# A transformer block on one core: the split for the fourth projected tile of a slot goes behind one more addition, and its cast waits for that addition

## The reference

```python
h = _ln(x, g1, be1)
x = _attn(h, h, Wq1, Wk1, Wv1, Wo1, bo1) + x     # self-attention
h = _ln(x, g2, be2)
x = _attn(h, context, Wq2, Wk2, Wv2, Wo2, bo2) + x
h = _ln(x, g3, be3)
y = h @ Wp + bp
a, gate = (y[..., :FF_HID], y[..., FF_HID:])
x = a * jax.nn.gelu(gate, approximate=False) @ W2 + b2 + x
```

## Time and profile before

| | |
|---|---|
| median of three runs | 2030.56 us (2029.66 to 2030.76) |
| the profiled execution | 2030.76 us, of which 2029.0 us are the span from first to last instruction |
| busy shares of the span | TensorE 99%, VectorE 69%, ScalarE 58%, GpSimd 73% |
| the six slots with projections | from 441 us to 1235 us |

### The profile page before, as it was taken

How to read it: one execution, slowest core, us unless ns; L and a number is a source line. 1 busy time by engine, 2 the same in 40 slices (tenths; PEclk the granted TensorE clock), 3 DMA queues, 4 the chain that set the end, 5 groups by cost and what they waited for, 6 DMA issues and landing times.

```text
span 2029.0 us, 32337 instructions
## 1 busy us (share of the span) xinstructions
PE 2015.9 (99%) x12692; PEld 1387.4 (68%) x12692; DVE 1392.1 (69%) x2128; ACT 1186.6 (58%) x1895; POOL 1476.3 (73%) x785
## 2 busy tenths in 40 slices
PE   8999999999999999999999999999999999999999
PEld 7665665667565566765665666565558999888888
DVE  5588677666767785577678566758777888744443
ACT  5566566665557675465667555557665666533332
POOL 2599899989979998999799889979894576300000
PEclk9999999999999999999999999999999999999999
DMA  7300000001000000010000001000020520000100
GB/s 230 125 27 22 6 6 16 6 27 48 16 12 6 17 7 27 1 63 6 6 6 22 26 1 52 6 27 1 22 60 5 146 84 1 1 22 22 42 11 32
DMA packets 48183, 64.01 MB, mean 32 GB/s; under 512 B 6048, under 2 KB 41504, under 8 KB 46368
## 3 DMA queue, kind: packets, MB, share of 16 engines
q1 hardware_dynamic: 48032, 61.96, 9.6%
HBM read 43.07 MB, written 18.87 MB: 31 GB/s over the span
## 4 chain that ended last, share of the span: by engine, by line
PE 96%; POOL 2%; issue 1%; ACT 1%; DMA 1%; DVE 0%; SPq 0%; POOLq 0%; ACTq 0%
PE score L516 21%; PE score L499 18%; PE score L641 9%; PE score L503 6%; PE attn_project L655 5%; PE score L447 4%; PE attn_project L627 4%; PE score L597 4%; PE attn_project L447 4%; PE first_score L473 3%; PE score L459 3%; PE attn_project L473 2%; PE score L565 1%; PE attn_project L459 1%; PE first_score L540 1%; PE attn_project L565 1%
## 5 line engine op out<-in xcount | busy, mean ns | idle before, releaser
L1392 POOL TENSOR_TENSOR acc<-acc,pT 128x1024 f32<-128x1024 f32 x384 | 916.2, 2386 | 53.6 <-POOL acc L1389 0.4
L1146 ACT ACTIVATE pT<-score 128x1024 f32<-128x1024 f32 x512 | 525.3, 1027 | 153.4 <-PE score L503 112.2
L499 PE MATMUL score<-qk 64*128 64x512 f32 x3072 | 457.2, 399 | 1.5 <-ACT oT L1159 0.9
L516 PE MATMUL score<-pT,vT 128*64 128x512 f32 x2016 | 446.5, 595 | 0.0
L818 DVE TENSOR_REDUCE nmax<-first_score 128x1 f32<-128x512 f32 x512 | 349.4, 682 | 4.8 <-PE first_score L473 2.9
L818 DVE TENSOR_REDUCE nmax<-attn_project 128x1 f32<-128x512 f32 x512 | 348.7, 681 | 0.0
L499 PEld LDWEIGHTS score<-qk 64*128 64x128 f32 x3072 | 257.8, 184 | 118.2 <-ACT pT L1146 65.9
L516 PEld LDWEIGHTS score<-pT,vT 128*64 128x64 f32 x2016 | 139.2, 137 | 289.3 <-issue 251.8
L840 DVE RECIPROCAL sums<-sums 128x512 f32<-128x512 f32 (+1 forms) x65 | 214.4, 3299 | 53.8 <-ACT sums L1193 53.2
L503 PE MATMUL score<-shift,pick 64*128 64x512 f32 x1024 | 206.2, 391 | 0.0
L1389 POOL TENSOR_TENSOR acc<-pT 128x1024 f32<-128x1024 f32 x64 | 154.0, 2406 | 68.9 <-ACT pT L1146 68.9
(11 more groups left out here) (170 smaller groups left out, 3086.9 us busy)
## 6 DMA issues: line engine op xcount, KB each, us to landing
xres<-x_middle SPq DMA_DIRECT2D x10, 512.0 KB, 3.8
xres<-in_x SPq DMA_DIRECT2D x4, 1024.0 KB, 8.7
raw_qk<-in_L_xattn_Wq SPq DMA_DIRECT2D x32, 128.0 KB, 2.3
raw_qk<-in_L_xattn_Wk SPq DMA_DIRECT2D x32, 128.0 KB, 2.4
raw_v<-in_L_xattn_Wv SPq DMA_DIRECT2D x8, 512.0 KB, 4.1
keys_all<-keys SPq DMA_DIRECT2D x1, 4096.0 KB, 12.1
values_all<-values SPq DMA_DIRECT2D x1, 4096.0 KB, 12.4
out_x<-xres SPq DMA_DIRECT2D x7, 512.0 KB, 2.9
```

The costliest lines, as they stand in the source:

```text
L499: e.matmul(bank, qk[P % 2][r, 2 + h, keys], qk[P % 2][r, w, queries], start=(part == 0), stop=False)
L516: last = e.matmul(banks[bank][head * DH:(head + 1) * DH, :], vT[:, v_slot(D, jt), c0:c0 + DH], pT[:, jt, head, :], start=(jt == 0), stop=( ...
L1146: e.activation(pT[:, jt].rearrange("p h n -> p (h n)"), SC[R % 2][:, :], ACT.Exp).then_inc(s.exponential, 1)
L1392: e.tensor_tensor(total, total, pT[:, jt], ALU.add).then_inc(s.probs_added, 1)
```

## The change

It has three parts, all for tile 3 of a slot. On ScalarE its cast, which waited for tile 0's projection alone, now also waits for `attended` at 8C + 7 and `probs_added` at 7C + 6. On GpSimd its subtraction waits for `attended` at 8C + 8 and no longer for tile 0's projection. And GpSimd does that subtraction after add 6 instead of after tile 2's.

```diff
@@ split_oT of ScalarE
-                if j < 3:
-                    need.wait_ge(s.attended, TILES * C + 2 * j + 1)
-                    need.wait_ge(s.probs_added, (TILES - 1) * C + max(2 * j, 1))
-                else:
-
+                need.wait_ge(s.attended, TILES * C + 2 * j + 1)
+                need.wait_ge(s.probs_added, (TILES - 1) * C + max(2 * j, 1))
+                if j == 3:
                     need.wait_ge(s.out1_product, TILES * b + t - j + 1)
@@ split_oT of GpSimd
                 need.wait_ge(s.oT_hi, TILES * b + t + 1)
-                if j < 3:
-                    need.wait_ge(s.attended, TILES * C + 2 * j + 2)
-                    need.wait_ge(s.probs_added, (TILES - 1) * C + 2 * j + 1)
-                else:
-                    need.wait_ge(s.out1_product, TILES * b + t - j + 1)
+                need.wait_ge(s.attended, TILES * C + 2 * j + 2)
+                need.wait_ge(s.probs_added, (TILES - 1) * C + 2 * j + 1 if j < 3 else 0)
@@ the loop of GpSimd over the chunks
-                    for tile in out1_tiles(C)[{4: slice(0, 2), 5: slice(2, 4)}.get(jt, slice(0, 0))]:
+                    for tile in out1_tiles(C)[{4: slice(0, 2), 5: slice(2, 3), 6: slice(3, 4)}.get(jt, slice(0, 0))]:
                         split_oT(C, *tile)
```

## The result

| | before | after |
|---|---|---|
| median of the runs | 2030.62 us (2029.66 to 2030.76, 4 runs) | 2047.11 us (2046.39 to 2049.41, 4 runs) |
| ratio, 95% interval | | 1.0084 [1.0066, 1.0102] |
| the profiled execution, its span | 2030.76 us, 2029.0 us | 2048.4 us, 2046.6 us |
| mean granted clock of TensorE | 1.000 | 0.997 |

The change costs 16.5 us, 0.8%. The forecast was 2045.2 in a range of 2041 to 2048.5. The median lies in the range, but the clock is not at 1.000 as forecast.

What follows compares the result with a forecast made beforehand. TensorE was taken as the bound; its new waits for tile 3's low part in six slots sum to 14.41 us, so 2030.76 + 14.41 = 2045.2 us, 0.7% slower, in a range of 2041 to 2048.5.

Steps and rivals of the forecast that it cites:

- TensorE bounds the stage and gives nothing back: Self-attention stage: TensorE waits only 2.5 us in all; at most 1.6 us could be regained, none taken.
- The rival of stalls given back: Score phase: ScalarE runs ahead after stalls, each chunk returning up to 1.3 us; not slower, 2030.8; chance 4%.
- The redundant conditions cost nothing: Tile 3's split: added waits for attend 7 or 8 cost nothing; dropping GpSimd's wait for tile 0's product gains nothing.
- The wait makes cast and subtraction serial behind add 6: Tile 3, six slots: cast and subtraction follow add 6 in turn, making TensorE 1.12 to 3.31 us late.
- The sum of 14.41: Lateness of tile 3's projection on TensorE in C = 17, 18, 33, 34, 49 and 50, 14.41 us together.
- What is late next: GpSimd after tile 3's subtraction: it falls less behind than TensorE, its V weights split does not wait; no second stall.
- The clock: Rival: TensorE's clock halves after gaps of about 3 us in C = 18, 34, 50; 8.6 more, 2053.8; chance 5%.

Runs made afterwards that it cites:

- the move alone: Changed kernel, but ScalarE's cast for tile 3 waits only for add 4 and tile 0's projection; 2036.60 us, ratio 1.0032.
- the run with the gap filled: Changed kernel plus 24 extra TensorE matmuls ahead of its wait for tile 3 in C = 18, 34 and 50; 2043.61 us, ratio 1.0066.
- the second slots: Kernel before, with the whole change only in C = 18, 34 and 50; 2042.41 us, ratio 1.0060.
- the redundant conditions undone: Changed kernel, but tile 3 waits for no `attended` and GpSimd's subtraction again for tile 0's projection; 2047.10 us, ratio 1.0084.
- first slots alone: Kernel before, with the whole change only in C = 17, 33 and 49; 2034.60 us, ratio 1.0021.
- a third filled: Changed kernel plus 8 extra TensorE matmuls ahead of its wait for tile 3 in C = 18, 34 and 50; 2045.83 us, ratio 1.0078.

## Why the prediction was right, and where it was not

*TensorE bounds the stage and gives nothing back.* Right. Lateness and slow matmuls, counted from the starts, account for the growth of the span to 0.1 us. The rival of stalls given back is refuted: the weight loads waited 64.8 us in 362 waits for exponentials in the changed kernel, against 65.9.

*The redundant conditions cost nothing.* Right, by the run that undoes them (2047.10 against 2047.11).

*The wait makes cast and subtraction serial behind add 6.* Right in mechanism: the cast's releaser is the add. With the move alone 6.3 us remain.

*The sum of 14.41.* It measured 13.2. From the start of tile 2's subtraction to tile 3's projection in C = 17 I had 8.58 us; it took 458.89 - 450.48 = 8.41. The hand-over from the add to the cast was 0.03 and not 0.08, the one to TensorE 0.10 and not 0.14, and an operation of GpSimd follows the one before it 0.03 before that one's recorded end. Six times 0.2 is the difference.

*What is late next.* Wrong in a detail that costs nothing. GpSimd's split of V weights does wait for the projection after C = 18 (1.32 us in the changed kernel), since the projection was slower than the 2.87 that I took. In the run with the gap filled, where it was not slow, GpSimd goes from the scaling to that split without a pause. GpSimd is behind nobody there.

*The clock.* This step failed. I gave the fall 5% and took none; it happened, in three of three long stalls of the profiled execution, at 5.7 us in all. My price of 8.6 was near it in kind, a projection at half speed, but only in C = 34 was nearly all of the projection slow. The argument against it was the 3.27 us of idle time before the first matmul, with the clock at 1.00 in the window around it. I misread that. The timeline of before goes on like this:

```profile
5.19 6.11 PE L391 MATMUL score<-ctxT,wkv 128*128 128x256 f32 x16 [0.38 <-DVE ctxT L790]
11.14 1.89 PE L391 MATMUL attn_project<-ctxT,wkv 128*128 128x256 f32 x8
12.87 1.89 PE L391 MATMUL score<-ctxT,wkv 128*128 128x256 f32 x8
```

The first 16 matmuls take 11.14 - 5.19 = 5.95 us, 0.37 each. The next ones, of the same line and shape, take (12.87 - 11.14) / 8 = 0.22 each. Seen singly, those that start at 7.06, 7.49 and 7.92 are 0.43 apart, twice 0.22. So TensorE ran at half speed there, up to about 10 us, although the windows report a clock of 1.00 for it. Traffic is no rival: the DMA engines' busy share was 0.91 from 5 to 10 us and 0.88 from 10 to 11, where the pace was full again. The trace of before thus showed a low clock after TensorE had stood idle, and spoke for the fall and not against it, and the chance of 5% rested on a column that the matmuls contradict. What a gap in the midst of steady matmuls does, that trace could not say: the longest within the run was 0.8 us.

The Trainium skill ("TensorE: Matmul & The Clock Gate", section "Why this matters for your kernels") advises against gaps of about this length; the stalls of 2.7 to 5.4 us here bear it out, 14 times in 15. Two of three gaps of 1.8 to 2.0 us, shorter than those it warns of, brought the fall as well. The prediction held the first gap of the trace against this advice; the slow matmuls behind that gap take the objection away.

That the median of 2047.11 lies in the range, and only 1.9 above the forecast, is luck in good part: the case that came about is the rival that I had put at 2053.8, outside the range. In the profiled execution the waits were 1.2 shorter than forecast, the start of the kernel 1.4 faster, and the slow matmuls, which I had left out, cost 5.9 with the 0.2 of the first slots; that execution was 1.3 slower than the median. 2045.2 - 1.2 - 1.4 + 5.9 - 1.3 = 2047.2.

What stays open: what decides whether the clock falls. In the traces named here it stayed up after 8 gaps of 0.2 to 1.7 us (the move alone, and the first slots of the changed kernel), fell after 2 of 3 gaps of 1.8 to 2.0, after 8 of 9 of 2.7 to 2.9 (the changed kernel, the second slots, the redundant conditions undone), and after all 6 of 3.3 to 5.4. The first slots of four other runs (first slots alone, gap filled, a third filled, redundant conditions undone) add 12 gaps of 0.8 to 1.5 us, none with a fall: tile 3's projection took 3.0 us after each. The length of the gap is thus not all, since 2.94 passed once and 2.03 did not, and in one execution of one kernel 2.04 passed in C = 34 and 2.03 did not in C = 50. What else counts was not tried.

## What to carry to other kernels

When a change makes the bounding engine wait, add the waits up from starts in the timeline, and price separately what a gap does to TensorE's clock afterwards: here 3.2 us by the run that filled the long gaps, and 5.7 in the profiled execution, on top of 13.2 of waits. Before calling the effect unlikely, look for a trace that has such gaps, and hold the clock that the profile reports against the distance between the starts of equal matmuls. And place a wait at the first instruction that reads the data: moving the wait for the low part two terms down was worth more (13.2 us) than removing the condition that made it late (10 us).

## What was unexpected of the hardware

TensorE gained 3.2 us by doing 72 needless matmuls in time that it would have stood idle. Eight needless ones in each of the three stalls instead of 24, which left gaps of 1.8 to 2.0 us, saved 0.5 us (1.3 by the bare medians), with the clock still falling after two of three. The fall begins at different points: in C = 34 of the changed kernel with the first matmul after the stall, in C = 18 of the second-slot run only with the second group of eight (its 24 matmuls took 498.35 - 493.94 = 4.41 us), and in C = 34 of that run not at all.
